# Image 0's selective scan inside the sampling stage, the third norm with it, and corners summed by two additions

## The reference

```
x = x + L0(gn(x))      # weights from relative positions, softmax over a 7x7 window, weighted sum
x = x + L1(gn(x))      # 3x3 convolution
x = x + L2(gn(x))      # deformable 3x3 convolution: offsets and mask from a 3x3 convolution,
                       # four corners sampled bilinearly for each of 9 taps, product with reg_w
x = x + L3(gn(x))      # two mamba branches (plain and shuffled channels), layer norms, product with W_p
```

```
u  = silu(conv4(x @ W_in.T) + conv_b)
dt = softplus((u @ W_x.T)[:, :4] @ W_dt.T + b_dt);  B, C = the other 32 columns of u @ W_x.T
h  = exp(dt * A) * h + (dt * u) * B          # one step for each position, A = -exp(A_log)
y  = sum over the 16 states of h * C, plus u * D_skip;  out = (y * silu(z)) @ W_out.T
```

## Time and profile before

| | |
|---|---|
| median of 3 runs | 6257.39 us (6249.47 to 6259.31) |
| span of the profiled execution | 6244.6 us |
| median less that span | 12.8 us |
| granted clock of PE, mean | 0.81 |
| busy share PE, DVE, ACT, POOL | 71%, 80%, 41%, 79% |
| stages: load and mixing; sampling; third norm; mamba | to 742; 742 to 3135; 3142 to 3168; from 3168 us |

### The profile page before, as it was taken

The page is one execution under the profiler, slowest core; times in us unless marked ns, Lnnn a source line. Parts: engine busy times, 40 slices in busy tenths (PEclk is TensorE's granted clock), DMA queues, the critical chain, the costliest instruction groups (busy, mean ns, idle before and its releaser), DMA issues. The chain is left out here.

```text
span 6244.6 us, 55481 instructions
## 1 busy us (share of the span) xinstructions
PE 4411.3 (71%) x14922; PEld 2398.8 (38%) x14922; DVE 5012.8 (80%) x3958; ACT 2533.4 (41%) x3949; POOL 4904.1 (79%) x3492
## 2 busy tenths in 40 slices
PE   3777656565555657463338888888888888888887
PEld 1566523332323233232214444444444444444443
DVE  5899736776766676666639999999999999999998
ACT  2222111111111111110026666666766766766664
POOL 1777627777777777777719999999999999999997
PEclk8887766656565656655569999999999999999999
DMA  6666623444434443443324544454454544444443
GB/s 165 133 135 136 139 79 104 123 114 145 123 104 133 127 123 105 135 116 114 104 79 149 165 157 154 161 162 148 160 163 147 169 151 156 160 153 162 155 152 120
DMA packets 379240, 855.17 MB, mean 137 GB/s; under 512 B 195672, under 2 KB 238576, under 8 KB 374580
## 3 DMA queue, kind: packets, MB, share of 16 engines
q1 hardware_dynamic: 294228, 619.96, 33.3%
q0 software_dynamic: 84672, 231.32, 12.4%
HBM read 768.83 MB, written 56.48 MB: 132 GB/s over the span
## 5 line engine op out<-in xcount | busy, mean ns | idle before, releaser
L863 POOL DMA_INDIRECT fl_quad<-table,fl_idx x1764 | 1697.3, 962 | 695.0 <-issue 536.7
L2097 POOL TENSOR_TENSOR ma_hc<-ma_h,ma_cc 128x784 f32<-128x784 f32 x1024 | 1882.2, 1848 | 235.8 <-DVE ma_h L1998 203.7
L1642 PE MATMUL ma_bank<-ma_hc,ident 128*128 128x392 f32 x4096 | 1528.0, 495 | 10.2 <-POOL ma_hc L2097 7.6
L1998 DVE TENSOR_TENSOR_SCAN ma_h<-ma_da,ma_state,ma_bank 128x784 f32<-128x784 f32 x768 | 1418.0, 1846 | 101.6 <-DVE ma_bank L1985 3.5
L1014 DVE TENSOR_TENSOR fl_part<-fl_quad,fl_bank 128x2304 f32<-128x2304 f32 x196 | 500.1, 2552 | 710.1 <-DMA fl_quad<-table,fl_idx 696.6
L1867 ACT ACTIVATE ma_da<-ma_dt,ma_a_neg 128x784 f32<-128x784 f32 x1024 | 948.2, 943 | 271.1 <-DVE ma_h L1998 176.6
L1985 DVE TENSOR_TENSOR ma_bank<-ma_dtu,ma_bank 128x784 f32<-128x784 f32 x1024 | 983.4, 960 | 80.5 <-PE ma_bank L1629 79.1
L1155 PE MATMUL fl_bank<-ident,fl_tap 128*128 128x128 f32 (+1 forms) x980 | 242.3, 409 | 937.4 <-DVE xres L1032 876.0
L1642 PEld LDWEIGHTS ma_bank<-ma_hc,ident 128*128 128x128 f32 x4096 | 705.3, 189 | 449.5 <-POOL ma_hc L2097 36.0
L1022 DVE TENSOR_REDUCE fl_tap<-fl_part 128x576 f32<-128x2304 f32 x196 | 796.5, 4064 | 0.1
L1629 PE MATMUL ma_bank<-ma_bc,ma_sel 96*128 96x512 bf16 (+1 forms) x2048 | 514.8, 333 | 376.2 <-DVE ma_h L1998 361.0
(11 more groups left out here) (229 smaller groups left out, 6131.6 us busy)
## 6 DMA issues: line engine op xcount, KB each, us to landing
ma_cc<-c_rows SPq DMA_DIRECT2D x512, 784.0 KB, 4.3
mx_win<-flat SPq DMA_DIRECT2D x64, 878.0 KB, 10.3
fl_quad<-table,fl_idx POOLq DMA_INDIRECT x1764, 2.7
table<-fl_xt SPq DMA_DIRECT2D x64, 392.0 KB
mx_mask<-in_c_mask SPq DMA_DIRECT2D x56, 294.0 KB, 4.5
ma_xs<-ma_x SPq DMA_DIRECT2D x64, 196.8 KB, 5.6
ma_xs<-ma_x SPq DMA_DIRECT2D x64, 196.5 KB, 6.1
mx_xf<-flat SPq DMA_DIRECT2D x8, 816.0 KB, 15.8
```

Source lines behind the costliest of these rows:

```text
L863: gp.indirect_dma_start(quad[i][:, kk, :], None, table, bass.IndirectOffsetOnAxis(ap=idx[i][:, kk:kk + 1], axis=0))\
L1642: ins = pe.matmul(ps_y[:, t, :], ident[:], hc[:, n % RH, at], start=False, stop=(n == DS - 1))
L1998: dve.tensor_tensor_scan(h[:, i % RH, :], da[:, i % RH, :], ps_bu[i % 2], before, ALU.mult, ALU.add).then_inc(scand, 1)
L2097: gp.tensor_tensor(hc[:, i % RH, :], h[:, i % RH, :], cc[:, i % (NGRP * GRP), :], ALU.mult)\
```

## The change

The scan of image 0 (NLITE = 1) leaves the mamba stage and is done between the tiles of the sampling stage, in 7 chunks of 448 columns with two branches each, so 14 sections of 16 units, 224 units. From tile 59 on each tile has one or two units, five in three tiles. Before that 13 pieces of an introduction stand in tiles 54 to 58. For a unit DVE now does three steps: product with B in PSUM, scan, and product with C, which PE spreads into a PSUM bank of its own (`spread_c`). B, C, y and the projections have one bank each; so the convolution, the offsets and the transposes of the preparation share one bank, and the transposes of the image come behind those of the offsets. `xres` holds two pairs instead of four, RQ is 3, `part` is a single buffer. The norm of each pair is done in slots 1 to 4 of the next pair, the last one after the last tile, and `stage_norm3` is gone. The corner sum is two additions. The mamba stage runs seven images.

```diff
+NLITE = 1
+LC = 448
+NLC = PIX // LC
-    RQ = 4
+    RQ = 3
+    NSECT = 2 * NLC * NLITE
+    NUNIT = DS * NSECT
+    FIRST = INTRO + (NINTRO + PERSLOT - 1) // PERSLOT
+    RATE = (5, 3)
-        part = [s_.sb(f"part{i}", [TS, 4, K2, CH]) for i in range(2)]
+        part = s_.sb("part", [TS, 4, K2, CH])
-        cps = [bank[:, 4 + i, :] for i in range(2)]
-        xps = bank[0:2 * PW, 6, 0:7 * CH].rearrange("p (a c) -> p a c", c=CH)
-        tps = bank[:, 7, 0:HT * M].rearrange("p (a m) -> p a m", m=M)
+        cps = bank[:, 2, :]
+        xps = bank[0:2 * PW, 2, 0:7 * CH].rearrange("p (a c) -> p a c", c=CH)
+        tps = bank[:, 2, 0:HT * M].rearrange("p (a m) -> p a m", m=M)
+        ps_b, ps_c, ps_y, ps_f = (bank[:, 4 + i, 0:LC] for i in range(4))
...
+        def units(T):
+            lo, hi = ((T + i - FIRST) * RATE[0] // RATE[1] for i in range(2))
+            return list(range(max(lo, 0), min(hi, NUNIT)))
...
             def corners(T):
                 e = T % 2
                 dve.wait_ge(scaled, START + T + 1)
+                dve.tensor_tensor(part[:, 0:2], part[:, 0:2], part[:, 2:4], ALU.add).then_inc(halved, 1)
+                dve.wait_ge(halved, START + T + 1)
                 if T >= 2:
                     dve.wait_ge(turned, START + T - 1)
-                dve.tensor_reduce(tap[e][:], part[e][:].rearrange("p s k c -> p k c s"), AX_X, ALU.add)\
-                   .then_inc(reduced, 1)
+                dve.tensor_tensor(tap[e][:], part[:, 0], part[:, 1], ALU.add).then_inc(reduced, 1)
...
             def tile(T):                       # DVE
+                own = units(T)
+                if own:
+                    times_b(own[0])
+                    scan(own[0])
                 scale(T)
+                if own:
+                    times_c(own[0])
+                    chain(own[0])
+                if own[1:]:
+                    times_b(own[1])
                 if T + RQ < NTILE:
-                    pick(T + RQ)
+                    take(T + RQ)
                 corners(T)
+                if own[1:]:
+                    scan(own[1])
                 if T:
                     add(T - 1)
+                if own[1:]:
+                    times_c(own[1])
+                    chain(own[1])
...
+            def spread_b(V):
+                S, n = divmod(V, DS)
+                if n == 0:
+                    pe.wait_ge(l_low, START + S + 1)
+                pe.wait_ge(l_scand, START + V)
+                pe.matmul(ps_b, sel[:, n, :], lbc[S % 2][:], start=True, stop=True).then_inc(l_bready, 1)
+            def spread_c(V):
+                S, n = divmod(V, DS)
+                pe.wait_ge(l_hcd, START + V)
+                pe.matmul(ps_c, sel[:, DS + n, :], lbc[S % 2][:], start=True, stop=True).then_inc(l_cready, 1)
+            def gather_y(V):
...
+                pe.wait_ge(l_hcd, START + V + 1)
+                pe.matmul(ps_y, ident[:], lhc[V % 2][:], start=False, stop=(n == DS - 1)).then_inc(l_yd, 1)
+            def after_scan(V):
+                if V + 1 < NUNIT:
+                    spread_b(V + 1)
+                chain(V)
+            def after_c(V):
+                gather_y(V)
+                if V + 1 < NUNIT:
+                    spread_c(V + 1)
             def tile(T):                       # PE
+                own = units(T)
+                before = units(T - 1)
                 if T:
                     project(T - 1)
+                if before:
+                    after_c(before[-1])
+                if own:
+                    after_scan(own[0])
+                if own[1:]:
+                    after_c(own[0])
                 turn(T)
+                if own[1:]:
+                    after_scan(own[1])
...
-    NCHUNK = NQ * NB
+    NBM = NB - NLITE
+    NCHUNK = NQ * NBM
-            stage_norm3(nc, k, xres, gn3)
```

More of the change, by code:

```diff
@@ L1051, in _, with intro @@
+            def intro(i):
+                if i in (2, 5):
+                    scale_in(i // 3)
+                if i == 9:
+                    step(0)
+                if i == 10:
+                    left(0)
+                if i == 12:
+                    low(0)
+            dve.memset(wpg[:], 0.0)
+            dve.memset(lhc[0][:], 0.0)
+            dve.memset(vec[:, 6:7], EPS).then_inc(l_zeroed, 1)
             dve.memset(om[:], 0.0).then_inc(cleared, 1)
@@ L1057, in _, with quiet, pair @@
             dve.wait_ge(consts, START + 16 * (NLOAD + 1))
-            program(add_up, prepare, tile)
+            program(add_up, prepare, tile, normal, set_up, intro)
             add(NTILE - 1)
+            close(NSECT - 1)
+            out_scale(NCK - 1)
+            finish(NCK - 1)
+            for s in range(4):
+                normal(NPAIR - 1, s)
+            dve.wait_ge(norm_set, START + NPAIR)
         @block.tensor
         def _(pe):
-            def pair(e):
+            def quiet(T):
+                if T >= 0:
+                    pe.wait_ge(copied, START + T + 1)
+                    pe.wait_ge(added, START + T)
+            def pair(e, T):
                 pe.wait_ge(moments, START + (NSTAT + 1) * (e + 1))
@@ L1130, in add_up, with normal @@
                 if s == 1:
-                    pair(3 * q)
+                    pair(order(q, 0), slot_at(q, 0, s))
+            def normal(q, s):
+                if s == 0:
+                    pair(order(q, 3), slot_at(q, 3, s))
+                if s == 2:
+                    pe.wait_ge(ready, START + order(q, 3) + 1)
+                    quiet(slot_at(q, 3, s))
+                    for h in range(2):
+                        ins = pe.matmul(psn[:, 32 + 2 * h:34 + 2 * h], pick[:, h, :], gnc[:, q, :],
+                                        start=True, stop=True)
+                    ins.then_inc(norm_p, 1)
+                    pe.wait_ge(norm_set, START + q + 1)
+                if s == 3 and q == 0:
+                    own = image_rows(0)
+                    pe.matmul(ps_f[:, 0:1], mixc[own, :], gnc[own, 0, 1:2], start=True, stop=True)\
+                      .then_inc(l_cvec, 1)
             def prepare(q, h, s):
@@ new lines, in intro @@
+            def intro(i):
+                if i in (3, 6):
+                    affine(i // 3 - 1)
+                if i in (0, 3):
+                    keep(i // 3)
+                if i in (1, 4):
+                    root_in(i // 3)
+                if i == 6:
+                    take_u(0)
+                if i == 7:
+                    silu(0)
+                if i == 8:
+                    soft(0)
+                if i == 9:
+                    high(0)
+                if i == 11:
+                    mid(0)
+                if i == 12:
+                    for V in range(2):
+                        decay(V)
@@ L1257, in tile @@
             def tile(T):
-                e = T % 2
+                e, own = T % 2, units(T)
                 if T == 0:
                     spread_coef(0)
+                if own:
+                    unit(own[0])
                 if T + 1 < NTILE:
@@ L1263, in tile @@
                     spread_coef(T + 1)
+                if own:
+                    chain(own[0])
+                if own[1:]:
+                    unit(own[1])
                 act.wait_ge(turned, START + T + 1)
```

686 lines of the change are left out of this document (571 added, 115 removed).

## The result

The changed kernel takes 6294.56 us (median of 4 runs, 6293.60 to 6301.86), the kernel before 6254.74 us on the same chip (4 runs). The ratio is 1.0067, 95% interval 1.0052 to 1.0081. Forecast were 6278 us, a loss of 21 us; measured are 40. The bound that was forecast for the stretch with the units, DVE waiting for PE's spread of C, is the one that stands there.

What follows compares the result with a forecast made beforehand. POOL's gathers set the sampling stage's pace and DVE fills the mamba stage; -370 mamba, -8 norm and tail, +24 start, +8 introduction, +71 gather delay, +296 units' stretch make +21: 6278 us, range 6215 to 6360.

Steps and rivals of the forecast that it cites:

- The sign: Whole kernel: slower by 21 us; chances 0.46 faster, 0.11 within 0.2%, 0.43 slower.
- The wait for PE, the new bound: Units' stretch: DVE waits for PE's spread of C instead of gathers, 2.1 to 4.1 us a tile from the preparation.
- DVE's own work: Units' stretch: DVE's tile work, units, section steps and image preparation sum to 10.1 us a tile.
- The clock: Units' stretch: PE's granted clock near 0.83, three tenths at half level, giving 13.6 us a tile, +296 us.
- the prediction's own two ends: Units' stretch: DVE's loop takes 12.65 us a tile with PE at full clock and 15.7 at half.
- The gathers' delay: Sampling stage: the two corner additions hold up gathers by 1.2 us a tile, +71 us over the first 59 tiles.
- Rival 3: Sampling stage: the two additions do not hold up gathers, the 71 us go, 6207 us; chance 0.10.
- The signs named for this term: Changed profile: products 12.6 us apart before the scan begins, mean gather duration up from 0.96 to about 1.08 us.
- Rival 1: Units' stretch: PE near full clock, DVE's and POOL's limits meet at 12.9 us a tile, 6184 us; chance 0.28.
- Rival 2: Units' stretch: PE near half level, 15.2 us a tile, waits on PE's order dominate, 6493 us; chance 0.17.
- The turning point given: Units' stretch: the case of PE near half level decides from 13.45 us a tile.
- Mamba, start, tail: One mamba image removed, -370 us; later start, +24; third norm's stage removed against a new tail, -8.

Runs made afterwards that it cites:

- experiment 1: Changed kernel with PE's order alone altered: gathering of y and spread of C ahead of the preparation, second B's spread ahead of the projection; 6022.96 us.
- experiment 2: Changed kernel with the corners summed by the reduction again instead of two additions, single product buffer kept; 6573.72 us, ratio 1.0518.
- experiment 6: Changed kernel with six unread PE products ahead of each turn of the units' stretch, PE's order unchanged; 6211.07 us, ratio 0.9944.
- experiment 3: Kernel before with the corners summed by two additions, all else as it was; 6314.54 us, ratio 1.0103.
- experiment 4: Kernel before with the two additions, and DVE's 0.28 us addition to the image put ahead of them so they begin later; 6378.74 us, ratio 1.0206.
- experiment 7: Changed kernel with experiment 1's PE order and each image-preparation piece cut in two, second half in the next tile; 6003.30 us, ratio 0.9605.
- experiment 9: Kernel of experiment 7 with the first image's convolution and offset products alternating between two PSUM banks; 5984.59 us, ratio 0.9577.
- experiment 10: Kernel of experiment 9 with four unread PE products ahead of each turn of the stretch; 5989.02 us, ratio 0.9589.

## Why the prediction was right, step by step

- **The sign: right, by luck as much as by the sum.** The prediction itself gave a faster kernel 0.46 and a slower one 0.43. Two errors partly cancel: tiles 0 to 54 were put 47 us too dear, the stretch 73 us too cheap; the other rows cancel to within 1 us. What is left is the 27 us between +21 and +48. Of these the medians show only 19 (+40), because the 12.8 us between median and profiled span, carried over unchanged, belonged to one short execution of the kernel before; after the change they are 2.1. The two ranges that the prediction states (6215 to 6360, 6140 to 6430) both hold the measured time.
- **The wait for PE, the new bound: right.** Forecast was that waits for gathers vanish in the stretch and waits of the product with C stand there; 463 us do. Experiments 1 and 2 show it as a loop of DVE and PE: 2.2 us a tile more where 1.95 of work on DVE is added, 2.1 less where only PE's order is changed.
- **DVE's own work: right.** 10.1 us a tile forecast, 10.03 measured.
- **The clock: the term that was mis-sized.** "At a 13.6 us period and a clock near 0.83 its busy share is 0.7, which agrees with that line." The busy share was 0.73 and the clock 0.69. The row with 67% busy at 0.82 came from another stage, with other work on PE; with 73% busy at 0.69 here, the busy share of a stage doesn't give the clock of another. By the prediction's own two ends, 12.65 and 15.7, clock 0.69 (six tenths at half level) would have given 14.5 us and 0.79 in experiment 6 13.9; measured are 14.15 and 13.47, both some 0.4 below. So the slope held (0.68 us for 0.10 of clock, forecast 0.61) and the ends were a little high: at 0.69 they hold 4.4 us beside DVE's own work, and 4.1 were measured, 3.85 of them waits for PE. With ends that fitted, the forecast would have been further off.
- **The gathers' delay: mis-sized too, 1.2 us a tile forecast from the earlier trace rows, 0.33 measured before the units.** It was averaged over all phases and the second addition counted in full. By experiments 3 and 4 the loss is the phase alone, which over all phases of a 1.25 us period would be 0.6 us. And while POOL sets the pace the product starts when a gather has landed, so that in experiment 3 the additions begin 0.3 or 0.4 us into the next gather in 165 of 196 tiles. In the stretch the delay is 0.75 us a tile (gathers of 1.046 us against 0.963 in experiment 2), and there POOL has air for it. Rival 3 had no delay and 11.4 us a tile; measured are 11.77, so it falls, though its zero was nearer than the 1.2. The signs named for this term (12.6 us a tile before the units, gathers of 1.08 us) did not show: 11.77 us and 1.00 us, and 1.05 us in the stretch.
- **Rival 1** (PE near full clock, both limits meeting) did not occur, at this order. **Rival 2** (half level, 15.2 us) did not either; the kernel was a third of the way there from the forecast. The turning point given, 13.45 us a tile, was 0.3 us low: experiment 6 stands at 13.47 with its time 0.6% under that before, since the first tiles were cheaper than thought.
- **Mamba, start, tail: right.** They came to -376, +28 and -13 us, where -370, +24 and -8 were forecast. The introduction cost 22 us instead of 14: ACT's root stands behind three other steps in one slot, and DVE waits for it:

```profile
1579.29 0.63 DVE L1238 TENSOR_TENSOR fl_l<-fl_l,fl_lt 128x448 f32<-128x448 f32 x1 [11.28 <-ACT fl_lt L1765]
...
1598.15 0.62 DVE L1238 TENSOR_TENSOR fl_l<-fl_l,fl_lt 128x448 f32<-128x448 f32 x1 [12.54 <-ACT fl_lt L1765]
```

- **What the prediction took as given and should not have:** the written order on PE. It found the wait, sized it at 2.1 to 4.1 us a tile, and stopped there. That a 0.35 us instruction behind a 5 to 10 us piece is a matter of order and not of capacity was in its own numbers. Experiment 1 gained 272 us by it, seven times what the change cost, and with experiments 7 and 9 the change is worth 4.2% (5984.6 us) instead of costing 0.7%.

## What to carry to other kernels

When work is moved into a stage with air, look at where its short hand-overs stand in the in-order queue of the engine that feeds the busy one: put them ahead of long pieces that nobody waits for. (That cutting those pieces helps as well was not shown here.) A clock forecast from busy shares of other stages is worth a wide range. And a cost by contention depends on the phase when one of the two engines sets off the other: take it from rows of the same pairing, not as a mean over phases.

## What the runs showed of the hardware

- A VectorE addition with two operands in SBUF costs an indirect gather about as much as it starts late in POOL's cycle: 0.29 us for a start 0.3 us into the gather before, 0.96 us for 1.0. The gather already under way is untouched. The reduction, with one operand in SBUF, costs none: in the kernel before, the 746 gathers that run beside it and beside none of the preparation's whole-image passes take 0.945 us on average and 0.955 at most. Where a copy of indices released POOL just ahead of the addition, 73 times in the stretch of the kernel after, the gather took 1.79 us on average instead of 0.95, as here, where it again ends 0.82 us after the addition:

```profile
2217.28 1.35 DVE L1170 TENSOR_TENSOR fl_part<-fl_part 128x1152 f32<-128x1152 f32 x1
...
2217.64 1.81 POOL L1002 DMA_INDIRECT fl_quad<-table,fl_idx  x1 [1.54 <-DVE fl_idx L1156]
```

- PE's granted clock was higher where its waits were shorter (0.69 to 0.75 in experiment 1 with the same work in less time), and products added in its idle time raised it to 0.79 (experiment 6): there a kernel gains by work that nobody reads. With POOL as the pace the same trick raised it from 0.76 to 0.81 and gave nothing (experiment 10).
- A 0.17 us copy right behind a 2.56 us product costs DVE nothing: the next addition begins 2.59 us after the product's start with it and without it.
